# A fused four-layer transformer stack on one core: halves of turned queries summed by POOL in two early layers, gated values read by ScalarE, and another order of all steps

## What is computed

```
x = x + attn_a(layernorm(x))     # l = 0: causal, 16 heads of 16, rotary positions on Q and K
x = x + ffn(layernorm(x))        # l = 1: gated
x = x + attn_b(layernorm(x))     # l = 2: 16 heads of 64, relative bias
x = x + ffn(layernorm(x))        # l = 3: gated, same weights as l = 1

# ffn: gate = sigmoid(t @ Wg); the 256 tokens of 512 with the highest gate are picked,
# attend to each other (16 heads of 16, no mask), pass Wo, are scaled by their gate
# and written back to their places; the other tokens get 0.
```

## Time and profile before

| | |
|---|---|
| three executions | 2005.8, 2005.87, 2006.48 us |
| the profiled execution | 2006.36 us, its span 2004.6 us |
| granted TensorE clock, mean | 0.997 |
| PE busy | 97% of the span, 15743 matmul records |
| PE weight loads busy | 62% |
| DVE, ACT, POOL busy | 74%, 57%, 36% |
| chain that ended last, by engine | PE 80%, DVE 11%, ACT 4% |

### The profile page before, as it was taken

How to read it: one execution, slowest core, us unless ns; L and a number is a source line. 1 busy time by engine, 2 the same in 40 slices (tenths; PEclk the granted TensorE clock), 3 DMA queues, 4 the chain that set the end, 5 groups by cost and what they waited for, 6 DMA issues and landing times.

```text
span 2004.6 us, 41582 instructions
## 1 busy us (share of the span) xinstructions
PE 1950.8 (97%) x15743; PEld 1244.9 (62%) x15743; DVE 1486.9 (74%) x4786; ACT 1152.3 (57%) x2588; POOL 714.4 (36%) x897
## 2 busy tenths in 40 slices
PE   8999999999999999999999999999999999999998
PEld 6666665656665666655666565665667556666566
DVE  8987666767879668877688677796877967856535
ACT  2554665475636766377553766457473675626753
POOL 5322324233433334333334333343333333404322
PEclk9999999999999999999999999999999999999999
DMA  4001211221201212112111122111220121212200
GB/s 171 2 2 43 72 64 45 66 69 44 76 23 62 75 41 69 38 46 98 41 56 46 36 90 59 38 47 52 80 68 26 62 69 33 76 34 81 71 12 12
DMA packets 37749, 110.02 MB, mean 55 GB/s; under 512 B 3696, under 2 KB 17648, under 8 KB 37424
## 3 DMA queue, kind: packets, MB, share of 16 engines
q1 hardware_dynamic: 34576, 103.43, 15.6%
q0 software_dynamic: 2976, 3.93, 1.1%
HBM read 97.39 MB, written 9.96 MB: 54 GB/s over the span
## 4 chain that ended last, share of the span: by engine, by line
PE 80%; DVE 11%; ACT 4%; issue 2%; DMA 2%; POOL 1%; POOLq 0%; DVEq 0%; ACTq 0%
PE ps L1036 24%; PE ps L1845 11%; PE ps L1837 10%; PE ps L1855 9%; PE ps L1603 9%; DVE peaks L1533 4%; PE ps L1797 3%; DVE ps L1448 3%; PE ps L1700 3%; PE ps L1686 3%; PE ps L1785 2%; ACT PTc L1294 2%; PE ps L1662 2%; DMA xg<-kept,tokens 2%; PE ps L1763 1%
## 5 line engine op out<-in xcount | busy, mean ns | idle before, releaser
L1228 POOL TENSOR_SCALAR probs<-probs,rtotal 128x512 f32<-128x512 f32 x512 | 359.2, 734 | 483.4 <-DVE rtotal L1559 483.4
L1338 ACT ACTIVATE probs<-probs,peak 128x512 f32<-128x512 f32 x512 | 365.0, 714 | 194.7 <-DVE peak L1555 194.6
L1550 DVE CUSTOM_DVE_ANT_0 probs<-ps,band 128x512 f32<-128x512 f32 x512 | 332.6, 687 | 60.8 <-PE ps L1837 60.7
L1347 ACT ACTIVATE PT<-ps 128x512 f32<-128x512 f32 x512 | 265.7, 621 | 48.8 <-PE ps L1845 48.0
L1845 PE MATMUL ps<-ident,probs 128*128 128x128 f32 x2048 | 250.3, 274 | 3.7 <-DVE peaks L1448 3.1
L1845 PEld LDWEIGHTS ps<-ident,probs 128*128 128x128 f32 x2048 | 225.8, 141 | 45.0 <-issue 34.1
L1448 DVE CUSTOM_DVE_ANT_0 ps<-ps,later 128x512 f32<-128x512 f32 (+3 forms) x512 | 232.8, 525 | 19.7 <-PE ps L1662 19.2
L1837 PE MATMUL ps<-KT,QT 64*128 64x512 f32 x1024 | 244.3, 608 | 0.0
L1855 PE MATMUL ps<-PT,Vb 128*64 128x512 f32 x1024 | 241.1, 602 | 0.0
L1036 PE MATMUL ps<-xnT,wb 128*128 128x512 f32 x512 | 234.7, 599 | 1.3 <-ACT xnT L1257 0.6
L1294 ACT ACTIVATE PTc<-ps 128x384 f32<-128x384 f32 (+1 forms) x384 | 168.0, 552 | 61.1 <-PE ps L1686 59.8
(11 more groups left out here) (191 smaller groups left out, 3213.9 us busy)
## 6 DMA issues: line engine op xcount, KB each, us to landing
band<-in_band SPq DMA_DIRECT2D x64, 896.0 KB, 4.6
wb<-in_w_b SPq DMA_DIRECT2D x64, 384.0 KB, 3.0
x<-in_x SPq DMA_DIRECT2D x16, 256.0 KB, 4.7
out<-x SPq DMA_DIRECT2D x16, 256.0 KB, 2.2
kept<-xn SPq DMA_DIRECT2D x7, 512.0 KB, 5.0
cos<-in_cos SPq DMA_DIRECT2D x8, 256.0 KB, 2.7
sin<-in_sin SPq DMA_DIRECT2D x8, 256.0 KB, 3.1
wob<-in_wo_b SPq DMA_DIRECT2D x1, 1024.0 KB, 8.5
```

The lines of the kernel that those rows point to most:

```text
L1228: last = g.tensor_scalar(unit, unit, rtotal[:, r % 8, e:e + 1], 1.0, ALU.mult, ALU.mult)
L1338: last = a.activation(unit, unit, ACT.Exp, bias=peak[:, r % 8, e:e + 1], accum_out=total[:, r % 8, e:e + 1])
L1347: a.activation(PT[:, k % 2, e, :, tile_of(q)], bank(now, name).rearrange("p (k n) -> p k n", k=NT), ACT.Copy).then_inc(act_read, 1)
L1550: v.tensor_tensor_reduce(out=probs[:, (r + LENT) % ROWS_HELD, e, :], in0=bank(now, name), in1=band[:, k % 2, e, lo:lo + T], scale=1.0, sca ...
```

## The change

- In two layers, (sample 1, l = 0) and (sample 0, l = 1), the sum of the query halves is a new step `c_xg`/`f_xg`: two plain additions of 128x512 on POOL in place of one 128x1024 instruction with a scalar on DVE. `sum_of(s, l)` tells which; in those layers ACT multiplies by 0 or -1 (column 3 of `sides`) and not by +1 or -1, which makes the sum the same. It concerns three steps: two of `c_xq`, one of `f_xq`.
- `f_v` of all sixteen gated layers is read from PSUM by ACT, no longer by DVE.
- The table `PLACE` is new nearly throughout, and one condition on when sample s + 1's first gated layer may reuse memory names four steps `f_p2` where it named one.

```diff
-    "f_q": [("o", "dve", 1)], "f_k": [("o", "dve", 1)], "f_v": [("o", "dve", 1)],
+    "f_q": [("o", "dve", 1)], "f_k": [("o", "dve", 1)], "f_v": [("o", "act", 1)],
...
+def sum_of(s, l):
+    return "xg" if (s, l) in ((1, 0), (0, 1)) else "xq"
...
-                side = add(held_back(ffn_steps(s + 1, 1), done), turned, [Step("f_p2", s - 1, 3, 3)])
+                side = add(held_back(ffn_steps(s + 1, 1), done), turned, [Step("f_p2", s - 1, 3, i) for i in range(4)])
...
-    ("cycle", "b_k"): [705, 371, 880, 1163, 1851, 1946, 2325, 2599],
+    ("cycle", "b_k"): [705, 575, 913, 1144, 1904, 1938, 2326, 2477],
...
+                        if kind in ("c_xg", "f_xg"):
+                            pool.wait_ge(signed_done, plan.after("signed", Step(kind[0] + "_rq", s, l, n), now))
+                            both, parts = pair_of(m, now)
+                            for e in range(2):
+                                half_of = slice(e * both.shape[-1] // 2, (e + 1) * both.shape[-1] // 2)
+                                last = g.tensor_tensor(parts[:, half_of], both[:, half_of], parts[:, half_of], ALU.add)
+                            last.then_inc(halves_q_done, 1)
...
+                        signs = sides[:, 3:4] if sum_of(s, l) == "xg" else sides[:, 0:1]
...
-                            a.activation(parts, both, ACT.Copy, scale=sides[:, 0:1]).then_inc(signed_done, 1)
+                            a.activation(parts, both, ACT.Copy, scale=signs).then_inc(signed_done, 1)
...
+                        if kind == "f_v":
+                            a.activation(m.Vxf[:, 0:NS * H * (DH + 1)].rearrange("p (h d) -> p h d", d=DH + 1)[:, :, 0:DH],
+                                         bank(now).rearrange("p (h d) -> p h d", d=DH), ACT.Copy).then_inc(act_read, 1)
...
-                        if kind == "f_v":
-                            v.tensor_copy(m.Vxf[:, 0:NS * H * (DH + 1)].rearrange("p (h d) -> p h d", d=DH + 1)[:, :, 0:DH],
-                                          bank(now).rearrange("p (h d) -> p h d", d=DH)).then_inc(dve_read, 1)
```

More of the change, by code:

```diff
@@ L265 @@
-    ("cycle", "f_k"): [170],
-    ("cycle", "f_ln"): [-107],
-    ("cycle", "f_m"): [365, 436],
-    ("cycle", "f_o"): [569],
-    ("cycle", "f_p1"): [320, -294, 345, 356],
-    ("cycle", "f_p2"): [380, 425, 396, 262],
-    ("cycle", "f_part"): [-4486],
-    ("cycle", "f_q"): [184],
-    ("cycle", "f_rank"): [40],
-    ("cycle", "f_row"): [-1],
-    ("cycle", "f_rq"): [-408],
-    ("cycle", "f_spread"): [94],
-    ("cycle", "f_v"): [219],
-    ("cycle", "f_va"): [462, 518],
-    ("cycle", "f_vb"): [-753, 405],
@@ new lines @@
+    ("cycle", "f_k"): [227],
+    ("cycle", "f_ln"): [-340],
+    ("cycle", "f_m"): [359, 425],
+    ("cycle", "f_o"): [609],
+    ("cycle", "f_p1"): [342, -117, 344, 373],
+    ("cycle", "f_p2"): [396, 406, 394, 302],
+    ("cycle", "f_part"): [-461],
+    ("cycle", "f_q"): [176],
+    ("cycle", "f_rank"): [123],
+    ("cycle", "f_row"): [86],
+    ("cycle", "f_rq"): [-320],
+    ("cycle", "f_spread"): [-142],
+    ("cycle", "f_v"): [292],
+    ("cycle", "f_va"): [468, 520],
+    ("cycle", "f_vb"): [326, 341],
@@ new lines @@
+    ("cycle", "f_xq"): [325],
+    ("cycle", "f_y"): [638, 226],
+    ("cycle3", "f_add"): [5438],
+    ("cycle3", "f_gate"): [4733],
+    ("cycle3", "f_get"): [3472],
+    ("cycle3", "f_hk"): [3477],
+    ("cycle3", "f_hm"): [5164, 5302],
+    ("cycle3", "f_idx"): [4851],
+    ("cycle3", "f_k"): [5027],
+    ("cycle3", "f_ln"): [4711],
+    ("cycle3", "f_m"): [5210, 5203],
+    ("cycle3", "f_mk"): [-1246],
+    ("cycle3", "f_p1"): [5177, 5133, 5283, 5183],
+    ("cycle3", "f_p2"): [5288, 5394, 5165, -1834],
@@ new lines @@
+    ("first0", "f_q"): [1042],
+    ("first0", "f_rank"): [1053],
+    ("first0", "f_row"): [901],
+    ("first0", "f_rq"): [-778],
+    ("first0", "f_spread"): [1104],
+    ("first0", "f_v"): [1080],
+    ("first0", "f_va"): [1333, 867],
+    ("first0", "f_vb"): [1048, 1432],
+    ("first0", "f_xg"): [-3051],
+    ("first0", "f_y"): [1868, -1778],
+    ("first1", "c_dk"): [448, 666],
+    ("first1", "c_dq"): [445, 576],
+    ("first1", "c_hk"): [-3690, 760],
+    ("first1", "c_hm"): [868, -1400],
@@ new lines @@
+    ("last1", "f_gather"): [22927],
+    ("last1", "f_hk"): [14267],
+    ("last1", "f_hm"): [12713, 13639],
+    ("last1", "f_idx"): [22955],
+    ("last1", "f_k"): [13015],
+    ("last1", "f_ln"): [22648],
+    ("last1", "f_m"): [22216, 23167],
+    ("last1", "f_mk"): [22840],
+    ("last1", "f_p1"): [12714, 13024, 22189, 22244],
+    ("last1", "f_p2"): [14281, 22926, 13640, 13011],
+    ("last1", "f_part"): [14281],
+    ("last1", "f_q"): [14281],
+    ("last1", "f_rank"): [22804],
+    ("last1", "f_row"): [22746],
@@ new lines @@
+    ("last1", "f_rq"): [12560],
+    ("last1", "f_sc"): [22666],
+    ("last1", "f_v"): [23765],
+    ("last1", "f_va"): [23080, 22723],
+    ("last1", "f_vb"): [23931, 22744],
+    ("last1", "f_xq"): [24738],
+    ("last2", "f_add"): [13746],
+    ("last2", "f_gate"): [20341],
+    ("last2", "f_get"): [20592],
+    ("last2", "f_hk"): [20081],
+    ("last2", "f_hm"): [19245, 16505],
+    ("last2", "f_idx"): [20479],
+    ("last2", "f_k"): [20611],
+    ("last2", "f_ln"): [20081],
+    ("last2", "f_m"): [22628, 22178],
@@ new lines @@
+    ("last2", "f_mk"): [20081],
+    ("last2", "f_p1"): [12895, 21073, 21649, 20831],
+    ("last2", "f_p2"): [14281, 14281, 22743, 13641],
+    ("last2", "f_q"): [20611],
+    ("last2", "f_rank"): [20477],
+    ("last2", "f_row"): [20131],
+    ("last2", "f_rq"): [20223],
+    ("last2", "f_sc"): [23037],
+    ("last2", "f_turn"): [20131],
+    ("last2", "f_v"): [20669],
+    ("last2", "f_va"): [22744, 22924],
+    ("last2", "f_vb"): [22758, 14275],
+    ("last2", "f_xq"): [20670],
+}
+def sum_of(s, l):
+    return "xg" if (s, l) in ((1, 0), (0, 1)) else "xq"
@@ L494, in ffn_steps @@
 def ffn_steps(s, l):
+    add = sum_of(s, l)
     def f(what, n=0):
```

378 lines of the change are left out of this document (155 added, 223 removed).

## The result

Four executions of the kernel after took 2067.79, 2068.59, 2069.31 and 2069.51 us, median 2068.95; the kernel before, run beside it, 2006.17 us. The ratio is 1.0311 (95% interval 1.0293 to 1.0329), that is 63 us more. The prediction was 1996 us with a range of 1988 to 2003. The profiled execution took 2068.59 us.

A forecast was written before the change was run, and what follows sets the result against it. PE was taken to bound the kernel, as a conveyor. Mode changes -4.4, second `f_p2` -6.2, wait before `b_val` -0.9, fillers -0.6 and new waits +2.0 sum to -10.1 us: from 2005.9 to 1996 us, range 1988 to 2003.

The forecast's parts named there:

- the term for new waits: Anywhere on PE: a new order has waits the old didn't; 2 us more allowed (0 to 8).
- rival C: First gated layer, steady part: POOL's normalisations, scatters and low parts make `f_p1` wait; slower, 2010 us; chance 0.05.
- Changes of mode: PE, mostly steady part: 26 fewer switches between whole-array and partial use at 0.17 us each, 4.4 us less (3.9 to 5.2).
- The second `f_p2`: Last gated layer: its 1.03 us wait for DVE's maxima vanishes in six samples, 6.2 us less (bounds 0 and 6.2).
- rival A: Last gated layer: the wait moves to `b_tr` or the `b_row` behind it, for banks or ACT; 2002 us; chance 0.13.
- `f_turn`: Its wait for two fetches, 7.4 us in seven times: steps from `f_idx` are the same in both orders, 0.
- The wait before `b_val`: Steady part: 0.3 us lost after three `b_row`; half of six times that goes, 0.9 us less (0 to 1.8).
- `f_v` on ACT: Sixteen reads leave DVE, 9.6 us onto ACT; neither engine bounds in the steady part: 0.
- The sum on POOL: First samples: DVE relieved, gain 0 to 4.6 us; later first passes, loss 0 to 3.8 us; taken as 0.
- DVE and POOL in each other's way on SBUF: Six new POOL instructions could each hold up a DVE instruction; at most 6.6 us, left in the range alone.
- Fillers: PE's filler instructions: five fewer at 0.11 us each, 0.6 us less.
- Rival B: First samples, where DVE bounds: its 4.6 us come out in full, with other terms' upper ends; 1988 us; chance 0.08.

The follow-up runs named there:

- own_memory: Kernel after, order untouched, but the last gated layer's `of` lies in other columns than `xgT`, so ACT's read of `f_gather` needn't await the scatters: 1997.12 us, ratio 0.9957.
- own_pair: own_memory, but in the last gated layer the second `f_p2` stands right behind the first again, ahead of the two `b_tr`: 1998.62 us, ratio 0.9962.
- own_turn: own_memory with one step moved: the second `b_val` of pair 3 stands ahead of `f_turn`, not behind `f_v`, in each steady sample: 1991.64 us, ratio 0.9923.

## Why the prediction was wrong

**The step that failed** is the term for new waits, "I allow 2 us more (0 to 8)". It was sized by the small items of PE's list before, as if a new order could only bring more of the same. It brought one of 72 us. The move that did it was in sight: rival C names POOL's block of twelve normalisations and two scatters. But the prediction asked of the scatters only how long POOL is busy with them, 3.1 us, and who waits for POOL's next instruction (`f_p1`). It did not ask who waits for the scatters to land. That is ACT at the very next step, `f_gather`, by a wait that stands in the code before and never cost anything there, because 36 steps lay between. So C's place was right; its waiter, its point of decision and its price (2010 us, chance 0.05) were wrong. The slow clock that follows a PE wait of this length had no term at all; it added 15 us.

**Point by point**, with own_memory as the order without that wait:

- What bounds. PE as a conveyor, the time read from its starts: this held in own_memory, where a sample's period is 238.7 to 239.2 us in the steady part, 1.7 shorter than before, which is what the prediction gave.
- Changes of mode, 4.4 us less. No run measures them by themselves. An estimate from the two traces, with each pair of neighbouring instructions at its usual distance of starts, gives 2.9 us, 0.11 for each of 26 changes; other choices of what is usual give 2.4 to 4.2. So 0.17 may have been too much, but that is not shown.
- The second `f_p2`, 6.2 us less. The wait shrank from 1.03 to 0.58 us and did not vanish: 2.7 us less. The two `b_tr` that were to cover it carried it past DVE's maxima, but one of its four banks is now that of the first `b_tr`, and what comes last is ACT's read of it. That read stands in ACT's queue behind the four exponentials of the first `f_p2`; it is not the exponentials themselves that PE waits for, as I had put it for own_pair. This is the geometry of rival A, with half its price. PE and ACT in the kernel after:

```profile
747.76 0.39 PE L1802 MATMUL ps<-gX,gLO 32*128 32x256 f32 x4 [0.59 <-ACT PT L1367]
```
```profile
745.06 2.06 ACT L1338 ACTIVATE PTf<-ps 128x512 f32<-128x512 f32 x4 [4.01 <-PE ps L1802]
746.98 2.10 ACT L1367 ACTIVATE PT<-ps 128x512 f32<-128x512 f32 x4
```

- `f_turn`, no change: 7.4 us before, 7.9 after, 7.3 in own_memory. Right; and own_turn shows what one step there is worth.
- The wait before `b_val`, 0.9 us less: it went in full, 0.3 us in six samples, 1.7.
- `f_v` on ACT, 0: in the old order 3 us slower. In the new order it can't be priced by itself, since the order leans on it (17 us when undone): the prediction sought its cost in the bank and in ACT's queue, and not in what it frees, DVE's queue ahead of `f_xq`.
- The sum on POOL, 0 within 4.6 and 3.8: in the new order a gain of 1.7 us by the medians, not clear of 0; in the old one 5 us slower, beyond the bound, because the bound counted the sum's own length and not the queue behind it.
- DVE and POOL in each other's way on SBUF, kept in the range at up to 6.6 us: no run here measures it by itself, and the sum of own_memory needs no such term. The new order even took six of these meetings away: the sums of layer 1 that last 1.97 us in the kernel before, one in each sample of the steady part, have no counterpart in own_memory, where none lasts over 1.38 us. PE's list has no wait for them in either kernel.
- Fillers, 0.6 us less: their time went from 70.5 to 72.1 us, 1.6 more.
- Rival B, the start. DVE was relieved from 60 to 110 us as counted (47.31 to 45.10 us busy), but sample 2's `c_xt` starts at 323.4 us in own_memory and at 322.4 before. No gain there.
- The sum of these, with 2.9 for the changes of mode, is 5.7 us less, and own_memory is 9.0 us below the kernel before. The other 3 are open: small waits that no term named, or changes that cost more than 0.11.

So 1997 us for the order without its new wait against 1996 forecast is partly luck: the term of the second `f_p2` was 3.5 us too large, that of the mode changes perhaps too, and small ones were forgotten.

## What to carry to other kernels

When an order moves a DMA that reads on-chip memory, look for whoever writes that memory next, and count from the issue: all that stands ahead of the DMA in its engine's queue, the issue, the landing, and only then the writer's wait, with everything that is queued behind the writer. A wait that costs nothing in the old trace is not listed in it, so it must be sought in the code, for each step that comes closer to another. And an engine move costs or gains by the queue it stands in, not by its own length: the same two moves were worth between -5 and +17 us depending on the order around them.
